# Another order at the beginning of a half-step feed-forward kernel: zeros, indices, scale parts and their loads

## The reference

```python
x = x + 0.5 * ffn(layernorm(x))
x = x + attention(layernorm(x))
x = x + 0.5 * ffn(layernorm(x))

def ffn(xf):                       # the same packed weights both times
    Wg = dequant(gate_qweight, gate_scales, gate_qzeros, gate_g_idx)   # 512 x 1376
    Wu = dequant(up_qweight, up_scales, up_qzeros, up_g_idx)           # 512 x 1376
    Wd = dequant(down_qweight, down_scales, down_qzeros, down_g_idx)   # 1376 x 512
    return (silu(xf @ Wg) * (xf @ Wu)) @ Wd

def dequant(qweight, scales, qzeros, g_idx):
    # eight 4-bit numbers in each word: w[k, n] and z[g, n]
    return (w - (z + 1)[g_idx]) * scales[g_idx]
```

## Time and profile before

| | |
|---|---|
| median of 3 runs | 834.06 us (833.72 to 834.32) |
| the profiled execution | 834.31 us |
| its span, from the first to the last instruction | 832.5 us |
| busy: TensorE, its weight load | 816.9, 671.9 us |
| busy: VectorE, ScalarE, GpSimd | 493.2, 272.8, 251.2 us |
| mean granted clock of TensorE | 0.998 of full speed |
| first stretch, 0 to 20.8 us | TensorE busy share 0.5 |

### The profile page before, as it was taken

The page is one execution under the profiler, slowest core; times in us unless marked ns, Lnnn a source line. Parts: engine busy times, 40 slices in busy tenths (PEclk is TensorE's granted clock), DMA queues, the critical chain, the costliest instruction groups (busy, mean ns, idle before and its releaser), DMA issues.

```text
span 832.5 us, 10583 instructions
## 1 busy us (share of the span) xinstructions
PE 816.9 (98%) x3944; PEld 671.9 (81%) x3944; DVE 493.2 (59%) x809; ACT 272.8 (33%) x471; POOL 251.2 (30%) x203
## 2 busy tenths in 40 slices
PE   5999999999999999999999999999999999999998
PEld 4777778878888888788888888888878888888786
DVE  7899945766554544547766785546346644443452
ACT  3333433455111111333656871121123311211221
POOL 5555614752115061303064371062411200110100
PEclk9999999999999999999999999999999999999999
DMA  5998968865754532334053159544444155444131
GB/s 157 268 347 276 311 202 286 335 254 222 277 189 140 170 133 70 105 107 152 1 178 126 39 178 373 207 139 166 126 154 154 43 197 170 133 150 153 29 102 51
DMA packets 73405, 143.04 MB, mean 172 GB/s; under 512 B 26092, under 2 KB 37028, under 8 KB 68362
## 3 DMA queue, kind: packets, MB, share of 16 engines
q1 hardware_dynamic: 66964, 131.10, 46.4%
q10 hardware_dynamic: 5526, 7.04, 2.4%
q0 software_dynamic: 864, 4.23, 1.8%
HBM read 104.30 MB, written 37.98 MB: 171 GB/s over the span
## 4 chain that ended last, share of the span: by engine, by line
PE 94%; DVE 2%; DMA 1%; POOL 1%; issue 1%; SPq 1%; ACT 1%; DVEq 0%; POOLq 0%
PE ps L811 52%; PE ps L804 38%; PE ps L822 2%; PE ps L1198 2%; DMA qs<-in_L_ffn_up_qweight 1%; DVE xn L1741 1%; SPq L561 1%; POOL wp L2213 0%; DMA zq_gu<-in_L_ffn_up_qzeros 0%; DVE stats L1718 0%; PE ps L890 0%; PE ps L1123 0%; POOL wd L2213 0%; DVE pT L1707 0%; ACT pr L1562 0%
## 5 line engine op out<-in xcount | busy, mean ns | idle before, releaser
L804 PE MATMUL ps<-blk,ring 128*128 128x512 f32 (+1 forms) x1386 | 321.2, 390 | 0.6 <-DVE u L1710 0.5
L804 PEld LDWEIGHTS ps<-blk,ring 128*128 128x128 f32 (+1 forms) x1386 | 256.5, 185 | 59.2 <-issue 1.2
L811 PE MATMUL ps<-wd,hT 128*128 128x512 f32 (+1 forms) x1056 | 251.7, 391 | 0.2
L811 PEld LDWEIGHTS ps<-wd,hT 128*128 128x128 f32 (+1 forms) x1056 | 196.9, 188 | 42.7 <-DVE h L1877 0.5
L2265 POOL TENSOR_TENSOR h<-h,u 128x512 f32<-128x512 f32 (+1 forms) x33 | 42.7, 1293 | 322.9 <-ACT h L1446 322.9
L811 PE MATMUL ps<-xT,wp 128*128 128x512 f32 x480 | 112.8, 391 | 0.2 <-POOL wp L2213 0.2
L811 PEld LDWEIGHTS ps<-xT,wp 128*128 128x128 f32 x480 | 89.8, 188 | 19.9 <-issue 0.6
L1710 DVE TENSOR_TENSOR u<-ps,p1s 128x512 f32<-128x512 f32 (+1 forms) x66 | 45.4, 687 | 97.0 <-PE ps L804 97.0
L1446 ACT ACTIVATE h<-h 128x512 f32<-128x512 f32 (+1 forms) x33 | 20.9, 632 | 177.7 <-DVE h L1710 177.7
L1710 DVE TENSOR_TENSOR h<-ps,p1s 128x512 f32<-128x512 f32 (+1 forms) x33 | 22.8, 691 | 64.3 <-PE ps L804 64.3
L1710 DVE TENSOR_TENSOR u<-ps,u 128x512 f32<-128x512 f32 (+1 forms) x66 | 45.6, 691 | 25.3 <-PE ps L804 24.3
(11 more groups left out here) (130 smaller groups left out, 887.2 us busy)
## 6 DMA issues: line engine op xcount, KB each, us to landing
ring<-wsaved SPq DMA_DIRECT2D x29, 1024.0 KB, 5.1
ring<-wsaved SPq DMA_DIRECT2D x33, 768.0 KB, 4.3
wsaved<-wp SPq DMA_DIRECT2D x10, 1024.0 KB, 5.2
stream<-xres SPq DMA_DIRECT2D x32, 256.0 KB, 2.3
xn<-stream SPq DMA_DIRECT2D x8, 1024.0 KB, 6.8
xres<-stream SPq DMA_DIRECT2D x32, 256.0 KB, 3.5
wfull<-wf ACTq DMA_DIRECT2D x20, 256.0 KB
wsaved<-wp SPq DMA_DIRECT2D x10, 512.0 KB, 4.9
```

The source lines that it names most:

```text
L804: mm = pe.matmul(ps[0:w, bank, :], ring[:, slot, which, a, kt, 0:w], blk[:, which, b, kt, :], start=not onto and kt == 0 and n == 0, stop= ...
L811: mm = pe.matmul(bank_ap, lhs(a), rhs(b), start=first and n == 0, stop=last and n == 2)
```

## The change

Nothing of the computation changes, but where and when some of it is done:

- SyncE loads down's zeros `zq_d` first, ahead of gate's and up's zeros. VectorE unpacks them first, too, ahead of gate's and up's; the wait before `zb_gu` counts both (`ZERO_STEPS` is now 19).
- GpSimd issues the two loads of `idx_d` and the one of down's scales to `rows_d`, behind its memset and a wait for VectorE's constants; SyncE issued them before. The gathers' waits follow.
- The clamp of `idx` is GpSimd's, behind these issues and ahead of the first `rstd`; VectorE waits for it (`s_idx`) and does the first comparison ahead of `ln_shift` of the last two row tiles instead of behind it.
- TensorE turns two of x's row tiles ahead of the scales of tile 0, the other two behind them; a `keep_warm(1)` goes.
- ScalarE sends the six scale parts in three pairs: part 0 ahead of unit 0's high part, part 1 behind unit 1's, part 2 behind unit 2's, that is in the first turn of `plain_top`. Before, all six went behind unit 1's.

```diff
--- before.py
+++ after.py
@@ -473,7 +473,7 @@
 
 
         FIRST_STEPS, PART_STEPS = 3, 7
-        ZERO_STEPS, ZERO_D_STEPS, TAB_STEPS = PACK + 2, 2 * PACK + 3, 2 * PACK + 4
+        ZERO_STEPS, TAB_STEPS = 2 * PACK + 3, 2 * PACK + 4
 
         FLAT_LOADS, PART_LOADS = 32, 128
 
@@ -637,12 +637,12 @@
                     sp.dma_start(as_kept(i, chip), kept(i, parts)).then_inc(d_ring[slot_of(n)][part], 16)
 
 
+            sp.dma_start(zq_d, flat(zeros[2], ZC_D)).then_inc(d_zq_d, 16)
             for m in range(2):
                 sp.dma_start(zq_gu[m * ZP:(m + 1) * ZP, :], flat(zeros[m], ZC)).then_inc(d_zq_gu, 16)
             for m, rows in enumerate((slice(0, Z_UP), slice(Z_UP, S_ROWS.stop))):
                 sp.dma_start(idx[rows, GU_COLS], spread(g_idx[m], rows.stop - rows.start)).then_inc(d_idx_gu, 16)
             sp.dma_start(grp[:, :], groups).then_inc(d_grp, 16)
-            sp.dma_start(zq_d, flat(zeros[2], ZC_D)).then_inc(d_zq_d, 16)
             sp.dma_start(idt[:, :], ident).then_inc(d_small, 16)
             sp.dma_start(shift[:, :], shifts).then_inc(d_small, 16)
             for m in range(2):
@@ -651,17 +651,8 @@
             sp.wait_ge(s_cut, 1)
             for m, row in enumerate((Z_ROW, Z_UP)):
                 sp.dma_start(zb_gu[row:row + GK, :], zs_gu[m][m * ZP:(m + 1) * ZP, :]).then_inc(d_zb, 16)
-
-            sp.wait_ge(s_cst, 4)
-            last = (NT - 1) * P
-            sp.dma_start(idx_d[:, 0:NT - 1], g_idx[2][0:last].rearrange("(i p) -> p i", p=P),
-                         allow_slow_non_contiguous=True).then_inc(d_idx_d, 16)
-            sp.dma_start(idx_d[0:INTER - last, NT - 1:NT], g_idx[2][last:INTER].rearrange("(p o) -> p o", o=1)).then_inc(d_idx_d, 16)
-            sp.dma_start(rows_d[:, 0:HID], scales[2]).then_inc(d_rows, 16)
-            load_units(sp, [1])
-            sp.wait_ge(s_tab, ZERO_D_STEPS)
             sp.dma_start(rows_d[:, HID:D_ROW].bitcast(BF16), zb_d).then_inc(d_rows, 16)
-            load_units(sp, [2])
+            load_units(sp, [1, 2])
             load_units(sp, [3, 4, 5])
 
 
@@ -1086,11 +1077,10 @@
             pe.wait_ge(d_small, 32)
             keep_warm(8)
 
-            pe.wait_ge(s_oh, 3)
-            scales_zeros(0)
             for r in range(RT):
                 if r == 2:
-                    keep_warm(1)
+                    pe.wait_ge(s_oh, 2)
+                    scales_zeros(0)
                 pe.wait_ge(s_ln[0], r + 1)
                 for k in range(KT):
                     mm = pe.transpose(ps[:, 4 + k, r * P:(r + 1) * P], xn0[:, 0, r, k * P:(k + 1) * P], idt[:, :])
@@ -1327,6 +1317,13 @@
                     bank = TURN_BANK[k] if t else 4 + k
                     copy((xT0, xT1)[t][:, 0, k, :], ps[:, bank, :]).then_inc(s_rhi, 1)
 
+            def send_parts(n):
+
+                act.wait_ge(s_cut, PART_STEPS)
+                for m in range(2):
+                    row = FOLD * m + GK * n
+                    act.dma_start(tab_rest[row:row + GK, :], sc_part[n][SP_ROWS * m:SP_ROWS * (m + 1), :]).then_inc(d_cut_rest, 16)
+
             def w_hi(u):
                 if u >= UNITS:
                     return
@@ -1367,6 +1364,8 @@
                         act.wait_ge(s_hlo, i - 1)
                     act.activation(hs[0:w, i % 2, :], ps[0:w, plain_bank(0, i, 0), :], ACT.Silu).then_inc(s_silu, 1)
                     w_hi(3 * i + 2)
+                    if i == 0:
+                        send_parts(2)
                     if i == 9:
                         ln_apply(1, (0, 1))
                     w_hi(3 * i + 3)
@@ -1526,15 +1525,12 @@
 
             ln_apply(0, (0, 1))
             ln_apply(0, (2, 3))
+
+            send_parts(0)
             w_hi(0)
             rows_hi(0)
             w_hi(1)
-
-            act.wait_ge(s_cut, PART_STEPS)
-            for m in range(2):
-                for n in range(3):
-                    row = FOLD * m + GK * n
-                    act.dma_start(tab_rest[row:row + GK, :], sc_part[n][SP_ROWS * m:SP_ROWS * (m + 1), :]).then_inc(d_cut_rest, 16)
+            send_parts(1)
             plain_top()
             rows_hi(1)
             plain_bottom()
@@ -2014,6 +2010,8 @@
                       lambda: dve.memset(idx_d[:, :], 0))
             for row in (0, FOLD):
                 constants(lambda: dve.memset(keep[row:row + 2 * GK, 1:2], 0.0), lambda: dve.memset(keep[row:row + GK, 0:1], 0.0))
+            dve.wait_ge(d_zq_d, 16)
+            unpack_zeros(dve, tables, zq_d, zi_d, (zb_d, 1.0, 1.0))
             dve.wait_ge(d_zq_gu, 32)
             unpack_zeros(dve, tables, zq_gu, zi_gu, (zs_gu[0], 1.0, Z_LOW), (zs_gu[1], 1.0 + Z_BIAS, 1.0))
             ln_stats(0, (0, 1))
@@ -2021,13 +2019,10 @@
             ln_stats(0, (2, 3))
             ln_shift(0, (0, 1))
             ln_var(0, (2, 3))
-            dve.wait_ge(d_zq_d, 16)
-            unpack_zeros(dve, tables, zq_d, zi_d, (zb_d, 1.0, 1.0))
-            dve.wait_ge(d_idx_gu, 32)
-            clamp(dve, hots, GU_COLS, GK, S_ROWS)
-            ln_shift(0, (2, 3))
+            dve.wait_ge(s_idx, 1)
             dve.wait_ge(d_grp, 16)
             compare_low(dve, hots, GU_COLS, 0, oh_gu[S_ROWS, :], S_ROWS)
+            ln_shift(0, (2, 3))
             one_hot(dve, hots, GU_COLS, 0, oh_gu[S_ROWS, :], S_ROWS)
             dve.wait_ge(s_cut, FIRST_STEPS)
             table_gu(dve, tables)
@@ -2280,15 +2275,24 @@
             cutter = maker(pool, s_cut)
 
             cutter(lambda: pool.memset(zb_gu[Z_ROWS, :], Z_MARK))
+            pool.wait_ge(s_cst, 4)
+
+            last = (NT - 1) * P
+            pool.dma_start(idx_d[:, 0:NT - 1], g_idx[2][0:last].rearrange("(i p) -> p i", p=P),
+                           allow_slow_non_contiguous=True).then_inc(d_idx_d, 16)
+            pool.dma_start(idx_d[0:INTER - last, NT - 1:NT], g_idx[2][last:INTER].rearrange("(p o) -> p o", o=1)).then_inc(d_idx_d, 16)
+            pool.dma_start(rows_d[:, 0:HID], scales[2]).then_inc(d_idx_d, 16)
+            indices = maker(pool, s_idx)
+            pool.wait_ge(d_idx_gu, 32)
+            clamp(pool, indices, GU_COLS, GK, S_ROWS)
             pool.wait_ge(s_cst, 8)
             deviation(0, 0, 2)
             pool.wait_ge(d_cut_gu, 32)
             first_left_gu(pool, cutter)
             deviation(0, 2, RT)
-            indices = maker(pool, s_idx)
             pool.wait_ge(d_cut_rest, FLAT_LOADS)
             scale_parts(pool, cutter)
-            pool.wait_ge(d_idx_d, 32)
+            pool.wait_ge(d_idx_d, 48)
             indices(lambda: pool.tensor_scalar(idf_d[:, :], idx_d[:, :], -float(GD), GD - 1.0, ALU.max, ALU.min))
             indices(lambda: pool.tensor_scalar(neg_d[:, :], idf_d[:, :], 0.0, float(GD), ALU.is_lt, ALU.mult))
             indices(lambda: pool.tensor_tensor(out=idf_d[:, :], in0=idf_d[:, :], in1=neg_d[:, :], op=ALU.add))
@@ -2299,7 +2303,7 @@
                 w_lo(u)
                 m, i = unit(u)
                 if u < 2:
-                    pool.wait_ge(d_rows, 32)
+                    pool.wait_ge(d_rows, 16)
                     gather(u)
                 if m == 2 and i + 2 < NT:
                     gather(i + 2)
```

## The result

The changed kernel took 835.74 us (median of 11 runs, 834.86 to 838.06), the kernel before, on the same chip, 834.12 (11 runs, 833.17 to 835.25). The ratio is 1.0024, with a 95% interval of 1.0014 to 1.0033: slower by about 1.6 to 2.0 us. The forecast was 834.4, so it was 1.3 us too low; the range (832.8 to 838.2) holds the time. "Within 0.2%" had 0.60 and "slower" 0.36: by the medians the difference is 1.62 us, just inside the bound of 1.67, and by the ratio just beyond it, on the slower side.

What follows compares the result with a forecast made beforehand. TensorE, 98% busy, was taken as the bound, restarting 5.8 us after the later of gate's product 1 (27.5) and `tab_rest` (28.2): 34.0 against 33.71, +0.3 us, so 834.4 against the median; range 832.8 to 838.2.

Steps and rivals of the forecast that it cites:

- Down's zeros first: VectorE's opening: x's statistics reached 0.7 us later, between 0.5 and 1.4; most of down's unpacking hidden in a wait.
- GpSimd's loads: GpSimd's opening: issuing the three loads takes 3.0, 1.0 and 1.0 us, leaving GpSimd free at 7.1.
- Rival (b): GpSimd's issue of single words takes longer than 3 us: 836.7 at 6.0 us, 841.0 at 10.2; chance 0.25.
- The clamp: On GpSimd ahead of the first `pow`: starts at 7.1, takes 1.6 us, so `pow` starts at 8.7 instead of 7.31.
- D: Delay of VectorE's unpacking from unit 0 on: 0.8 us, from 1.4 of later `pow` less 0.6.
- Turning two rows first: TensorE's transposes ahead of tile 0's scales: worth 0, as tile 1 waits for unit 2's low part anyway.
- SyncE's queue and unit 3: Units 1 to 5 load 1.8 us earlier, unit 3's last issue ends at 16.4; weights' chain 1.3 us earlier.
- The last pair: ScalarE's last scale parts behind unit 2: issue ends at 24.1, `tab_rest` lands 4.1 us later, at 28.2.
- rival (c): Last pair lands 6.6 us after its issue: +2.8, 836.8 us; it decides from 5.5 on; chance 0.10.
- rival (d): TensorE's clock stays at the lower level into gate's and up's first products: +3.3, 837.4 us; chance 0.03.
- A: Theory of the experiments: the last pair of scale parts, sent behind unit 2, makes `tab_rest` late and TensorE waits.
- C: Theory of the experiments: GpSimd's three loads stand among the start's small loads (`shift`, `grp`, `idx`), which then land late.

Runs made afterwards that it cites:

- a_again: The changed kernel again, word for word, beside the kernel before on another chip; 835.4 us, ratio 1.0012.
- e5: The changed kernel with down's zeros loaded and unpacked at their old places; 834.95 us, ratio 1.0006 to the kernel before.
- f4: The kernel before with only the new order of zeros, down's first; 834.79 us, ratio 0.9995.
- e1: The changed kernel with all six scale parts sent together behind unit 1's high part again; 835.25 us, ratio 1.0007 to the kernel before.
- e4: The kernel before with only the loads of down's indices and scales moved to GpSimd; 834.08 us, ratio 0.9994.
- e3: The changed kernel with the three loads of down's indices and scales back on SyncE; 834.95 us, ratio 1.0008 to the kernel before.
- f1: The kernel before with only the scale parts sent in three pairs, the last behind unit 2; 835.03 us, ratio 1.0007.
- e2: The changed kernel with the clamp of the indices back on VectorE; 835.71 us, ratio 1.0017 to the kernel before.
- e7: The kernel before plus GpSimd's three loads, two rows turned ahead, scale part 0 sent before unit 0's high part, 1 and 2 behind unit 1's; 833.67 us, ratio 0.9988.
- e6: The changed kernel with the six scale parts together behind unit 1 and the three loads on SyncE again; 834.78 us, ratio 1.0001 to the kernel before.
- f3: The kernel before with two rows turned ahead, scale part 0 sent before unit 0's high part, 1 and 2 behind unit 1's; 834.75 us, ratio 0.9999.

## Why the prediction was near, and where it was wrong

**Down's zeros first**: named 0.7 us later at VectorE's statistics, measured 1.4 (0.6 in a_again). The unpacking itself took 0.87 and lay whole in the gap, as said. Up's zeros came later than the 0.47 of their place in the queue: ready 5.28 against 3.88. What stood at the upper bound was the load, not the work. No cost of it can be measured (e5, f4).

**GpSimd's loads**: 3.0, 1.0 and 1.0 named, 1.21, 0.59 and 0.55 measured. Rival (b), with 0.25, fell: the lower bound, the gather's 1.0, was the near one. The clamp's start was near (7.1 named, 7.45 measured) by luck: GpSimd was free at 4.6, not at 7.1, and `idx`, named for the same 7.1, is what it waited for. "DMA: Bandwidth & Descriptors", section "Anatomy of one DMA", of the Trainium skill says that many descriptors can be emitted before the cost shows: the trace agrees in the main, as 1280 words took 1.21 us and 96 words 0.59, thirteen times the words for twice the time.

**The clamp**: `idx` landed at 7.45 (7.1 named), and it took 1.95 us (1.6), over the bound of 1.86. `pow` came at 9.48 instead of 8.7, unpacking of unit 0 at 14.51 instead of 13.7; the 5.0 us between the two held exactly. "GPSIMD Engine Reference", section "Engine selection", of the Trainium skill has one-input work on this engine as roughly line rate; 1.95 us against VectorE's 0.42 for the same elements speaks against it here.

**D, the delay of the weights: the first step that failed.** It was forecast as 0.8 and measured at 2.3 where tile 0's weights take their scales (15.81 against 13.51). 0.8 of the difference is the later `pow`; the other 0.7 is a wait of VectorE for TensorE (0.82 in the row at 15.81) that wasn't in the sum. Turning two rows first was costed at nothing because their eight transposes would be hidden. But they also stand ahead of tile 0's scales, behind the sixteen `keep_warm` products, and these wait for `shift`. It landed at 9.77 instead of 7.8. How much of it shows then hangs on the transposes: with `shift` at 9.77, 9.65 and 9.60 (the changed kernel, e1, a_again) the eight took 1.92, 1.68 and 1.23 us, and VectorE waited 0.82, 0.53 and 0.15. So the 0.7 is of the one profile, and a_again has little of it. The prediction moved none of the loads that stayed ahead in SyncE's queue but up's zeros and `idx`; `shift` and `grp`, issued while GpSimd's three were in flight, came later too (`shift` 9.02 with the loads alone in e4, 7.40 with them gone in e3; `idx` at 6.79 in e3 against 7.45). It counted what each queue lost, not what the others gained as neighbours.

**SyncE's queue and unit 3**: unit 3's last issue ended at 17.05 (16.4 named), since the loads behind the unpacked zeros began 0.9 us later, at 6.74 against 5.88, not 0.4; and the wait of 2.13 us was gone, as said. D of 2.1 at that point used it all up.

**The last pair: the second step.** Its place was right and so was the mechanism, but for sizes. Issue ended at 25.35 (24.1 named; 1.25 of late weights), landing came 5.3 after it (4.1 named), so `tab_rest` was there near 30.7, the upper end of the range given, instead of 28.2. The reason given for the 4.1 points the wrong way: SyncE's loads of units being further on was to make the landing quicker, but in the four profiles where they are it took 5.0 to 5.4 us, and in the two where they aren't 3.9 (e3) and at most 3.7 (f1). In f1, on the old order, the forecast of the issue held (24.15). This is rival (c) by another road: it asked for a landing 5.5 us after the issue and got 5.3 plus the later issue.

**The clock**: rival (d) had 0.03. Its mechanism is there in four of the nine profiles with the new order of rows, at a smaller size: 1.6 us where it hits gate's and up's first products (7.32 against 5.70 in a_again, the same in e2 and e5), 1.2 on up's product of tile 1 in the profile above. How many of the runs without a profile have it isn't known; 57 of 98 have a mean clock as low as these four. The wait for the table behind it hides a part: in e2 the first products took 1.64 us more than in e1 and began 0.83 earlier, and gate's product of tile 2 started at 34.88, 0.17 later. But it also sends the last pair later, as a_again shows.

**The sum**: 34.0 was named for gate's product of tile 2, 37.61 measured in the longest run. By its own terms: 2.5 from `tab_rest` (1.25 issue, 1.2 landing), 0.9 from the low clock behind the idle time; the remaining 0.15 is the short wait for GpSimd's low part ahead of 33.71, which the 5.8 of the sum left out. In the runs as a whole the loss is +2.0 on the mean (first set; +1.6 by the medians) and +0.9 (a_again), against +0.3 named: the direction and the last pair as the bound were right, the size was not.

What the runs settle: undoing the last pair and the loads together takes the loss away (1.0001, and faster than the changed kernel on the same chip), and undoing the clamp leaves most of it. Undoing one of the two gives 1.0007 or 1.0008. That A and C share the loss is read from the traces and fits these ratios, but with intervals of 0.0009 to either side the single shares aren't resolved. Why the first set gives 1.0024 and the second 1.0012 for one kernel stays open. Whether the order of the small loads in the DMA engines or the engines' load makes `shift` late wasn't tried apart.

## What to carry to other kernels

A load moved to another queue doesn't leave the DMA engines: here the small loads that the old queue issued from then on landed later, so look up which of them has a first waiter that the same change has moved onto the path. A transfer hung behind the last of several dependent steps inherits the lateness of all of them; send it earlier, as soon as its own input is ready and the queue has room, as e7 does. And work taken out of TensorE's waiting time may not be free: the kernels in which it left an idle stretch had runs with a lower mean clock more often, though what causes that isn't shown.

## What the runs showed of the hardware

- A load of single words, 1280 of them, is issued by GpSimd in 1.21 us in all seven profiles that have it; 96 words took 0.59 (0.94 in e7), ten rows of 2 KB 0.55 to 0.76.
- With those three in flight, `shift` (0.5 KB) took 4.9 to 6.0 us from its issue and `grp` 5.3 to 5.9, in the seven profiles that have them; in the seven without, 3.5 to 4.8 and 3.9 to 5.1.
- The last pair of scale parts, sent behind unit 2, was there 5.0 to 5.4 us after its issue's end in four profiles where SyncE's loads of units went out earlier, 3.9 and at most 3.7 us in the two where they didn't.
- GpSimd's one-input operation on 76x512 int32 took 1.93 to 1.95 us, 0.93 to 1.23 on 76x256 bf16; VectorE took 0.42 to 0.67 for the first.
- VectorE's unpacking of 128x512 int32 mostly took 0.48 us. Where a GpSimd operation on two tensors of 128x512 was already running as it began, it took 0.66 to 1.58 us and ended 0.3 us behind that operation, all 45 times in the first 60 us of the fourteen profiles (the changed kernel: 21.38 to 22.31, GpSimd's low part to 22.01). Where GpSimd's began after it (26.33 against 26.15), it took 0.48.
- TensorE's granted clock fell to the lower level behind idle stretches of 1.90 us (the changed kernel, 32 to 36 us) and 1.95 us (a_again, e2, e5), and didn't behind the same 1.95 us in the changed kernel's own profile nor in e1, e3, e6, e7 and f3.
